# A graph layer on one core: VectorE's order within a chunk, and six more picked tiles

## What is computed

```python
M_in = concatenate([x[src], edge_attr], axis=1)       # 200000 x 128
Y = relu(M_in @ M_W.T + M_b)                          # a message for each edge
Z = segment_sum(Y, dst, num_segments=6250)            # summed at the destination
h = relu(concatenate([x, Z], axis=1) @ U_W.T + U_b)
out = layernorm(x + h)                                # over the 64 features
```

## Time and profile before

| what | value |
|---|---|
| median of 3 runs | 1632.22 us |
| the profiled execution, its own time | 1629.82 us |
| its span | 1628.0 us |
| chunk loop, from the first transposes (chunk 0) to those of chunk 195 | 36.7 to 1595.4 us |
| picks / gathers issued from chunk 5 on | 264 / 1230 |

### The profile page before, as it was taken

The page is one execution under the profiler, slowest core; times in us unless marked ns, Lnnn a source line. Parts: engine busy times, 40 slices in busy tenths (PEclk is TensorE's granted clock), DMA queues, the critical chain, the costliest instruction groups (busy, mean ns, idle before and its releaser), DMA issues.

```text
span 1628.0 us, 55355 instructions
## 1 busy us (share of the span) xinstructions
PE 1551.1 (95%) x18721; PEld 1494.0 (92%) x18721; DVE 1436.2 (88%) x1609; ACT 352.6 (22%) x661; POOL 1213.5 (75%) x1292
## 2 busy tenths in 40 slices
PE   5899999999999999999999999999999999999997
PEld 5799989998999998999999999999998998999995
DVE  6899998898998898899989899889989888899885
ACT  4432122221221222122212212211221212212111
POOL 6777777777777777777777777777777777777774
PEclk9999999999999999999999999999999999999999
DMA  8332333333333333333333333323333323333332
GB/s 177 74 72 66 78 68 78 74 73 72 72 73 66 79 67 81 70 73 74 73 73 73 72 78 68 80 65 72 73 72 68 77 66 81 71 73 75 72 67 46
DMA packets 177463, 121.36 MB, mean 75 GB/s; under 512 B 106964, under 2 KB 155842, under 8 KB 177176
## 3 DMA queue, kind: packets, MB, share of 16 engines
q0 software_dynamic: 40640, 41.68, 14.1%
q1 hardware_dynamic: 105754, 56.86, 13.6%
q10 hardware_dynamic: 30782, 19.23, 5.0%
HBM read 114.44 MB, written 3.20 MB: 72 GB/s over the span
## 4 chain that ended last, share of the span: by engine, by line
POOL 42%; issue 22%; PE 15%; SPq 14%; DVE 4%; ACT 1%; DMA 1%; ACTq 0%; DVEq 0%
POOL gathered L429 42%; PE p_pick L1042 9%; SPq L395 9%; SPq L391 2%; DVE onehot_src L814 2%; PE p_messages L1025 1%; SPq L356 1%; PE p_messages L1049 1%; SPq L355 1%; PE p_edges_T L1007 1%; DMA edges<-in_edge_attr_dram 0%; PE p_pick L1100 0%; ACT block_start L524 0%; DVE XZ L755 0%; DVE gathered L776 0%
## 5 line engine op out<-in xcount | busy, mean ns | idle before, releaser
L429 POOL DMA_INDIRECT gathered<-Y_rows,src_all x1227 | 1158.0, 944 | 374.2 <-issue 370.9
L1042 PE MATMUL p_pick<-Y_parts,onehot_src 128*128 128x192 bf16 x12936 | 1104.4, 247 | 31.6 <-DVE onehot_src L814 16.1
L1042 PEld LDWEIGHTS p_pick<-Y_parts,onehot_src 128*128 128x128 bf16 x12936 | 1076.5, 98 | 39.9 <-issue 19.2
L814 DVE TENSOR_TENSOR onehot_src<-p_dve,block_start 128x6272 bf16<-128x6272 int16 x264 | 897.1, 3421 | 7.3 <-PE p_pick L1042 0.7
L1025 PE MATMUL p_messages<-w_edges,edges_T 128*128 128x128 f32 x1564 | 213.2, 279 | 4.3 <-ACT edges_T L550 4.2
L550 ACT COPY edges_T<-p_edges_T 128x512 f32<-128x512 f32 x196 | 114.7, 585 | 387.5 <-PE p_edges_T L1007 386.8
L564 ACT ACTIVATE match<-src_spread,minus_node 128x128 int16<-128x128 int32 (+1 forms) x190 | 84.1, 442 | 526.6 <-issue 526.6
L1025 PEld LDWEIGHTS p_messages<-w_edges,edges_T 128*128 128x128 f32 x1564 | 190.9, 192 | 5.7 <-ACT edges_T L550 3.9
L570 ACT ACTIVATE messages<-p_messages 128x512 f32<-128x512 f32 x196 | 116.9, 596 | 305.3 <-DVE p_messages L798 299.4
L798 DVE TENSOR_TENSOR p_messages<-p_messages,gathered 128x512 f32<-128x512 f32 x191 | 133.3, 698 | 50.9 <-DMA gathered<-Y_rows,src_all 26.5
L767 DVE SCALAR_TENSOR_TENSOR onehot<-p_dve,base,dst_all 128x576 f32<-128x576 f32 x195 | 157.5, 807 | 0.1
(11 more groups left out here) (120 smaller groups left out, 201.0 us busy)
## 6 DMA issues: line engine op xcount, KB each, us to landing
row_tile<-Y_rows SPq DMA_DIRECT2D x2560, 0.2 KB
edges<-in_edge_attr_dram SPq DMA_DIRECT2D x190, 192.0 KB
gathered<-Y_rows,src_all POOLq DMA_INDIRECT x1227
slow_tile<-Y_rows ACTq DMA_DIRECT2D x1152, 0.2 KB
edges<-in_edge_attr_dram SPq DMA_DIRECT2D x191, 64.0 KB
src_spread<-in_src_dram ACTq DMA_DIRECT2D x74, 128.0 KB
src_spread<-in_src_dram ACTq DMA_DIRECT2D x116, 64.0 KB
Y_rows<-Y SPq DMA_DIRECT2D x6, 256.0 KB
```

What stands on the lines that cost most here:

```text
L429: nc.gpsimd.indirect_dma_start(out=gathered[c % G][0:parts, j * D:(j + 1) * D], out_offset=None, in_=table, in_offset=bass.IndirectOffsetO ...
L814: nc.vector.tensor_tensor(onehot_src[k % SLOTS][:, :, :], sources.unsqueeze(1).to_broadcast([P, NW, P]), block_start[:, :, :], ALU.is_equa ...
L1042: last = nc.tensor.matmul(p_pick[k % 2][:, 0:3 * D], onehot_src[k % SLOTS][:, b, :], Y_parts[:, b, :], start=(b == 0), stop=(b == NW - 1))
```

## The change

```diff
     def picked_tiles(c):
         if not X <= c < NC:
             return []
-        return [TILES - 2, TILES - 1] if c % 9 in (0, 3, 6) or c % 18 == 8 else [TILES - 1]
+        return [TILES - 2, TILES - 1] if c % 3 == 0 or c % 18 == 8 or c % 36 == 5 else [TILES - 1]
...
                 for c in range(NC + 1):
                     for k in picks_of[c]:
                         sum_pick(k)
+                    if not narrow and c > 0:
+                        add_all_windows(c - 1)
+                    add_rows(c)
                     if narrow:
                         compare(c, base[:, c:c + 1])
-                        if c > 0:
-                            start_window(c - 1, columns)
-                    elif c > 0:
-                        add_all_windows(c - 1)
-                    add_rows(c)
-                    if narrow and c > 0:
-                        end_window(c - 1, columns)
                     if c < 2:
                         second_rest(c)
                     if c == X - 2:
                         dve.wait_ge(s_block_start, 2)
                     if picks_of[c + 2]:
                         copy_match(c + 2)
-                    for k in picks_of[c + 2]:
+                        compare_src(c + 2, picks_of[c + 2][0])
+                    if narrow and c > 0:
+
+                        start_window(c - 1, columns)
+                    for k in picks_of[c + 2][1:]:
                         compare_src(c + 2, k)
                     if narrow:
-
+                        if c > 0:
+                            end_window(c - 1, columns)
                         columns = window_columns(c)
```

## The result

| | before | changed |
|---|---|---|
| median of the runs | 1631.37 us (1627.76 to 1632.57, 4 runs) | 1649.07 us (1647.2 to 1655.8, 4 runs) |
| ratio to before, 95% interval | | 1.0107 [1.0076, 1.0138] |
| the profiled execution, its span | 1629.82, 1628.0 | 1647.63, 1645.8 |

The changed kernel is slower by 1.1%, 17.7 us. The forecast was 1642, with 1650 as the upper end: the sign held, the size was too small by 7 us. The measured time lies outside the forecast's own range, 1636 to 1647; the upper end of 1650 was there for a rival.

What follows compares the result with a forecast made beforehand. SyncE's full queue was taken as the bound, then TensorE's last 13 turns. Start 6.5, queue's run 0, last turns 5.2, end -0.5: +11.2 us, forecast 1642 us, own range 1636 to 1647, with rivals 1628 to 1650.

Steps and rivals of the forecast that it cites:

- the second rival: Pairs of adjacent doubles cost TensorE 3 us each, so it can't catch up with SyncE's queue: about 1655 us; chance 0.12.
- the slowest of the three, by 1%: Per 36 chunks: SyncE's queue needs 292.7 us, GpSimd's gathers 290, TensorE 279.8; so the queue sets the pace.
- The start: Chunk 5's extra pick delays the transposes of chunk 10 and SyncE's load of chunk 13: 6.5 us, between 3.5 and 7.
- the second pick of 5: Chunk 5 at the start: its added pick makes TensorE end at 71.4 instead of 67.95 us, +3.5.
- the wait: Ahead of chunk 6's picks, TensorE waits 3.0 us for VectorE's first sum of a pick of chunk 5.
- The order: New order of VectorE's steps: taken as 0 over the queue-bound stretch, between 0 and 3 us; 0.5 gained at the end.
- The wait of L819: VectorE's wait for TensorE's windows ahead of `add_rows`, 42.6 us in all: near zero after, worth 0 in the last turns.
- The queue's run: SyncE's queue from its load of chunk 13 to that of chunk 192: 1454 us, unchanged, term 0.
- The last turns: TensorE's last 13 turns, chunks 182 to 195: chunk 185's pick 4.04 plus 1.2 for the new pair, together 5.2 us.
- GpSimd's lead: At the end of the loop, the last gather comes some 10 us ahead of the loop's end.
- The gathers' gain (1): GpSimd, not SyncE's queue, sets the pace, so six fewer gathers save 7.5 us: about 1622 or 1624; chance 0.13.
- No change (3): The start's delay is made good by faster VectorE and the pair at 185 costs nothing: about 1635 us; chance 0.20.

Runs made afterwards that it cites:

- e5: Kernel before with half of SyncE's row DMAs, each writing one source's row to two rows; 1629.07 us, 0.9979 times before.
- e6: Changed kernel with half of SyncE's row DMAs, each writing one source's row to two rows; 1632.15 us, 0.9997 times before.
- e11: The changed kernel run once more, unaltered, for a second trace; one run, 1641.63 us.
- e7: Changed kernel with 34 unused matmuls filling TensorE's wait ahead of the picks of chunk 6; 1646.78 us, 1.0091 times before.
- e1: Changed kernel with the old pick condition (264 picks), so only the new order of VectorE's turn; 1630.68 us, 1.0005 times before.
- e2: Kernel before with the new pick condition (270 picks) and the old order of VectorE's turn; 1642.25 us, 1.0070 times before.
- e10: Kernel before with 80 doubles, none adjacent (270 picks), row DMAs still in every ninth chunk; median 1628.14 us, 0.9977 times before.
- e12: The kernel with 80 non-adjacent doubles and row DMAs in every ninth chunk, run again for a second trace; one run, 1630.42 us.
- e4: Changed kernel without the extra picks of chunks 5 and 185 (268 picks); 1631.97 us, 1.0018 times before.
- e3: Changed kernel without the extra pick of chunk 5 (269 picks); 1638.1 us, 1.0051 times before.
- e8: Kernel before, old order, with 83 doubles, none adjacent, and row DMAs in every tenth chunk instead of ninth; 1620.06 us, 0.9934 times before.

## Why the prediction came out as it did

**Luck.** The measured time lies inside 1628 to 1650 only because the upper end reached to the middle of the second rival, and that rival's price of 3 us a pair wasn't there. The terms of the forecast alone gave 1641.0 to 1643.4.

**The bound** was right in that the queue was full, halving its row DMAs gives the changed kernel 17 us, and the chain no longer holds gathers. But the distances to the others were too large. What the forecast had as "the slowest of the three, by 1%" was for the kernel before less than that: e5 shows the gathers behind it within 2 us. And TensorE with VectorE needs 290.0 us for 36 chunks (e6), not 283.8: the forecast counted picks and turns and left out the waits at the pairs and the lower clock behind some of them. In e11 TensorE waited for no edges behind chunk 146, so from there on the queue did not hold it up at all. The start and the last turns come out at the end by either bound, which is why the sum held up.

**The start** was the mis-sized term: 6.5 forecast, 9.2 measured, past the 7 that I had as its end. Its steps were right (the second pick of 5: 3.5 forecast, 2.8 measured; the wait: 3.0 and 3.09). I let the matmuls behind the wait keep their 8.25 us. They took 11.16, and 9.55 in e11; e7 shows that the idle time is behind it. Two waits of the kernel before gave no warning: behind 1.22 us the clock stayed, and behind the 2.95 us of the earlier trace rows too, whose next turn keeps its 6.20 us. But the same trace holds both outcomes behind waits of one size, at chunks 60 and 78:

```profile
502.94 8.24 PE L1042 MATMUL p_pick<-Y_parts,onehot_src 128*128 128x192 bf16 x98 [2.20 <-DVE onehot_src L814]
```
```profile
647.64 9.90 PE L1042 MATMUL p_pick<-Y_parts,onehot_src 128*128 128x192 bf16 x98 [2.20 <-DVE onehot_src L814]
```

Such a wait leaves both outcomes open, and I should have held the second one in the range of this term.

**The order** at 0 was right for the time (e1, 1.0005 [0.9987, 1.0023]) and wrong at the place: it costs 3.1 us at chunk 13 in e1, by a longer wait at the pair 8 and 9 and a lower clock behind it. I had written that the gap there doesn't grow. I looked at where `add_rows` gets earlier and not at what the moved window sums push back. In the full change the order's cost came at chunk 6 instead: against e2 it had gained 0.9 us ahead of that chunk, waited 0.9 us more there and lost 2.9 by the lower clock. The wait of L819 fell to 1.5 us, as forecast, and was worth nothing, as forecast: VectorE waits longer for TensorE at L776 instead.

**The queue's run** was forecast unchanged and measured at +2.2 in one execution and -2.3 in the other (e11). That is within what e10 and e12 show for one kernel. So the profiled execution's +17.8 us is 9.2 at the start, 3.2 between chunks 13 and 182, 5.9 in the last turns and -0.5 at the end; in e11 the span is 11.8 above before, near the sum's 11.2. How much of the 7 us between forecast and median is the clock, and how much the spread of the queue's run, these runs don't settle.

**The last turns**: 5.2 forecast, 5.9 measured, and 5.6 between e4 and e3. One pick of 4.04, 1.7 for the turn with the wait of 1.49 at the new pair, and 0.2 more than before at the pair 188 and 189.

**GpSimd's lead** of some 10 us at the end of the loop was wrong. The last gather ends at 1585.51 and the transposes of 195 start at 1613.68: 28 us.

```profile
1584.61 0.90 POOL L429 DMA_INDIRECT gathered<-Y_rows,src_last  x1 [0.30 <-issue]
```

Before, the lead was 2 us (1593.65 to 1595.40). I added the six gathers to it and forgot that the loop itself ends later by the very sum that I had just worked out.

**The rivals.** The gathers' gain (1) wasn't there, but its mechanism is real: when the queue is relieved and the pairs are gone (e8), the time falls to 1620 and the chain is one of gathers. Dearer pairs (2) fell as a price: it needed 3 us for each, and the page has 28.0 us of waiting for sums of picks in all, in 17 places, 1.65 each; only the one at chunk 6 reaches 3. Its direction was right: the pairs used up most of the slack that the forecast gave TensorE (2.7 us left of 8.9). No change (3) fell with both terms that it had to cancel.

## What to carry to other kernels

When two resources bind at the same spot, moving work from one to the other buys nothing; find both by relieving each alone (e5 the queue, a gain of 0.2%; e4 some of the gathers, no gain), then relieve them together. Here a third cost, the pairs, had to go with them: e6 relieves both, keeps the pairs and has six more picks, and is level with before; e8 takes away all three and is 0.66% faster. Where an engine needs a result of the step before the last, heavy steps placed side by side make it wait, so spread them evenly, and keep extra work out of the start and the end, where no slower resource covers it. A reordering that removes a wait of an engine that is ahead moves the wait to its next instruction.

## What the runs showed of the hardware

TensorE's granted clock fell behind a single wait inside a busy kernel, but not behind each. 98 matmuls that take 8.25 us took 9.91 behind 2.80 us of idle (e1), and 9.55, 9.91 and 11.16 behind 3.09 us (e11, e6, changed). e4 has both outcomes 145 us apart, two pairs of doubles in TensorE's timeline:

```profile
98.46 9.85 PE L1043 MATMUL p_pick<-Y_parts,onehot_src 128*128 128x192 bf16 x98 [2.56 <-DVE gathered L776]
```
```profile
243.15 8.26 PE L1043 MATMUL p_pick<-Y_parts,onehot_src 128*128 128x192 bf16 x98 [3.03 <-DVE gathered L776]
```

The shorter wait cost 1.6 us more in its matmuls, the longer one nothing. Over the loops of all fourteen traces, from chunk 5 on, each time that TensorE stood idle for 1 us or more, and how often its granted clock averaged under 0.90 in the 5 us behind it:

| idle, us | times | clock fell behind it |
|---|---|---|
| 1.0 to 1.5 | 90 | 0 |
| 1.5 to 2.0 | 66 | 14 |
| 2.0 to 2.5 | 27 | 15 |
| 2.5 to 3.0 | 14 | 13 |
| 3.0 to 4.4 | 14 | 13 |

No fall in these stretches came without such a wait. So a wait of 2.5 to 3.1 us nearly always costs 1.3 to 2.9 us more than itself, one of 2 us about every second time, and 34 filler matmuls kept the clock up in e7. And a queue that is never idle isn't a constant: 179 chunks took it from 1452 to 1461 us with the same number of DMAs, and the part that varied was the issue of the edge loads (158.3 and 168.6 us in e10 and e12), not that of the row DMAs (592.9 in both).
